# Eight additions of 256 elements in place of three on GpSimd, in the fold of a cross network's second layer

## What is computed

```python
x0 = xk = e                                  # [1024, 39, 16], gathered from 39 tables
for W in (f0, f1, f2):                       # [39*39,128], [128*39,128], [128*39,128]
    z = einsum('bfd,bgd->bfgd', x0, xk)      # every field with every row of the layer before
    cur = einsum('bpd,pm->bmd', z, W)        # 128 new rows
    outs.append(cur); xk = cur
h = concat([sum over d of each cur, dense_ctx])          # [1024, 400]
y = relu(relu(h @ W_top1 + b1) @ W_top2 + b2) @ W_top3   # [1024, 1]
```

## Time and profile before

| | |
|---|---|
| median of three runs | 1338.43 us |
| profiled execution | 1340.8 us |
| its span | 1339.0 us |
| matmul busy | 1281.1 us, 96% of the span |
| VectorE busy | 1149.6 us, 86% |
| ScalarE busy | 915.3 us, 68% |
| GpSimd busy | 1058.3 us, 79% |
| granted TensorE clock, mean | 0.99 of full speed |

### The profile page before, as it was taken

How to read it: one execution, slowest core, us unless ns; L and a number is a source line. 1 busy time by engine, 2 the same in 40 slices (tenths; PEclk the granted TensorE clock), 3 DMA queues, 4 the chain that set the end, 5 groups by cost and what they waited for, 6 DMA issues and landing times. The chain is left out here.

```text
span 1339.0 us, 25654 instructions
## 1 busy us (share of the span) xinstructions
PE 1281.1 (96%) x5983; PEld 1017.3 (76%) x5983; DVE 1149.6 (86%) x3210; ACT 915.3 (68%) x3053; POOL 1058.3 (79%) x743
## 2 busy tenths in 40 slices
PE   4899999999999999999999999999999999999998
PEld 2577777877788777887768877788767887788787
DVE  3499999699888999789986999969998699988983
ACT  2377776677666777577765777757776577766783
POOL 7588888688886888779887788868888688884561
PEclk9699999999999999999999999999999999999999
DMA  7623233322233322223332133330333322333000
GB/s 197 158 54 52 61 64 65 61 41 53 48 61 61 64 54 46 44 56 61 65 65 44 25 63 66 65 63 9 62 64 66 61 40 44 55 61 61 2 3 1
DMA packets 129470, 76.62 MB, mean 57 GB/s; under 512 B 90792, under 2 KB 98201, under 8 KB 129301
## 3 DMA queue, kind: packets, MB, share of 16 engines
q1 hardware_dynamic: 119061, 72.07, 26.5%
q0 software_dynamic: 10240, 2.64, 2.2%
HBM read 68.16 MB, written 3.87 MB: 54 GB/s over the span
## 5 line engine op out<-in xcount | busy, mean ns | idle before, releaser
L394 ACT ACTIVATE parts<-pieces,x_cols 128x128 f32<-128x128 f32 x2560 | 717.9, 377 | 188.3 <-PE pieces L690 159.4
L528 DVE SCALAR_TENSOR_TENSOR parts<-pieces,x_cols,parts 128x128 f32<-128x128 f32 x2432 | 678.7, 339 | 136.8 <-PE pieces L690 99.4
L688 PE MATMUL pieces<-w_hi,cur_hi 128*128 128x512 f32 (+1 forms) x1280 | 549.3, 429 | 29.2 <-DVE parts L528 23.0
L690 PE MATMUL pieces<-w_hi,cur_lo 128*128 128x512 f32 (+1 forms) x1280 | 499.4, 390 | 0.0
L689 PE MATMUL pieces<-w_lo,cur_hi 128*128 128x512 f32 (+1 forms) x1280 | 499.1, 390 | 0.0
L342 POOL TENSOR_TENSOR parts<-parts 128x1024 f32<-128x1024 f32 x127 | 324.2, 2553 | 149.8 <-DVE parts L528 144.4
L333 POOL DMA_INDIRECT emb<-in_table,rows x320 | 345.1, 1079 | 79.7 <-issue 60.9
L688 PEld LDWEIGHTS pieces<-w_hi,cur_hi 128*128 128x128 f32 x1280 | 242.1, 189 | 102.3 <-DVE parts L528 46.4
L690 PEld LDWEIGHTS pieces<-w_hi,cur_lo 128*128 128x128 f32 x1280 | 241.2, 188 | 51.7
L689 PEld LDWEIGHTS pieces<-w_lo,cur_hi 128*128 128x128 f32 x1280 | 242.3, 189 | 47.7
L413 ACT ACTIVATE pairs_hi<-pairs 117x512 fp32r<-117x512 f32 (+1 forms) x224 | 141.9, 634 | 190.9 <-DVE pairs L538 137.3
(11 more groups left out here) (66 smaller groups left out, 597.6 us busy)
## 6 DMA issues: line engine op xcount, KB each, us to landing
partners<-x_wide SPq DMA_DIRECT2D x62, 546.0 KB
partners<-x_wide SPq DMA_DIRECT2D x31, 468.0 KB
x_rep<-x_wide SPq DMA_DIRECT2D x96, 78.0 KB
emb<-in_table,rows POOLq DMA_INDIRECT x320
x_diag<-x_cols SPq DMA_DIRECT2D x256, 10.0 KB
x_wide<-emb SPq DMA_DIRECT2D x32, 80.0 KB
x_wide<-emb SPq DMA_DIRECT2D x32, 32.0 KB
wt<-in_wt SPq DMA_DIRECT2D x1, 1024.0 KB
```

The lines of the kernel that those rows point to most:

```text
L394: last = nc.scalar.activation(parts[n % 2][:, 4 * i + r, :], src[:, r * H:(r + 1) * H], ACT.Copy, scale=x_cols[n // 4][:, n % 4, f:f + 1])
L528: nc.vector.scalar_tensor_tensor(acc, src[:, r * H:(r + 1) * H], x_cols[n // 4][:, n % 4, f:f + 1], acc, ALU.mult, ALU.add).then_inc(acc_d ...
L688: nc.tensor.matmul(dst[:, 0:width], hi[:, cols], w1_hi[:, ws], start=True, stop=False)
L690: nc.tensor.matmul(dst[:, 0:width], lo[:, cols], w1_hi[:, ws], start=False, stop=True).then_inc(l2d_ready if q in D_PIECES else l2a_ready, 1)
```

## The change

GpSimd's three additions per block become eight of 256 elements per partition: four for the first step, in the order of slots 0, 4, 2, 6; two for the second, two for the third. The first four wait for nothing of each other. Each of the other four waits for the addition two places before it, in place of the one just before it. `tree_done` now rises by 8 per block. VectorE's fold of the last block keeps its three instructions and raises the semaphore by 4, 2 and 2. No number that is computed changes.

```diff
-TREE = 3
+TREE = 8
+FOLD = 2
...
-                pool.tensor_tensor(v[:, 0:8], v[:, 0:8], v[:, 8:16], ALU.add).then_inc(tree_done, 1)
-                pool.wait_ge(tree_done, g * TREE + 1)
-                pool.tensor_tensor(v[:, 0:4], v[:, 0:4], v[:, 4:8], ALU.add).then_inc(tree_done, 1)
+                for a in (0, 4, 2, 6):
+                    pool.tensor_tensor(v[:, a:a + FOLD], v[:, a:a + FOLD], v[:, a + 8:a + 8 + FOLD], ALU.add
+                                       ).then_inc(tree_done, 1)
+                for a in (0, 2):
+                    pool.wait_ge(tree_done, g * TREE + a + 2)
+                    pool.tensor_tensor(v[:, a:a + FOLD], v[:, a:a + FOLD], v[:, a + 4:a + 4 + FOLD], ALU.add
+                                       ).then_inc(tree_done, 1)
                 wait(pool, cur2_ready, g - 1)
-                pool.wait_ge(tree_done, g * TREE + 2)
-                pool.tensor_tensor(out4[:], v[:, 0:4], v[:, 16:20], ALU.add).then_inc(tree_done, 1)
+                for a in (0, 2):
+                    pool.wait_ge(tree_done, g * TREE + 5 + a // 2)
+                    pool.tensor_tensor(out4[:, a:a + FOLD], v[:, a:a + FOLD], v[:, a + 16:a + 16 + FOLD], ALU.add
+                                       ).then_inc(tree_done, 1)
```

More of the change, by code:

```diff
@@ L571, in add_last_parts @@
                 dve.wait_ge(acc_done, (g + 1) * D_OPS)
-                nc.vector.tensor_tensor(v[:, 0:8], v[:, 0:8], v[:, 8:16], ALU.add).then_inc(tree_done, 1)
-                dve.wait_ge(tree_done, g * TREE + 1)
-                nc.vector.tensor_tensor(v[:, 0:4], v[:, 0:4], v[:, 4:8], ALU.add).then_inc(tree_done, 1)
+                nc.vector.tensor_tensor(v[:, 0:8], v[:, 0:8], v[:, 8:16], ALU.add).then_inc(tree_done, 4)
+                dve.wait_ge(tree_done, g * TREE + 4)
+                nc.vector.tensor_tensor(v[:, 0:4], v[:, 0:4], v[:, 4:8], ALU.add).then_inc(tree_done, 2)
                 dve.wait_ge(cur2_ready, g - 1)
-                dve.wait_ge(tree_done, g * TREE + 2)
-                nc.vector.tensor_tensor(out4[:], v[:, 0:4], v[:, 16:20], ALU.add).then_inc(tree_done, 1)
+                dve.wait_ge(tree_done, g * TREE + 6)
+                nc.vector.tensor_tensor(out4[:], v[:, 0:4], v[:, 16:20], ALU.add).then_inc(tree_done, 2)
             def halve_tails(u, n):
```

## The result

The changed kernel takes 1384.2 us (median of 4, 1382.4 to 1388.8), the kernel before 1339.3 beside it (4 runs): ratio 1.034, 95% interval 1.031 to 1.037. The forecast was 1354, 16 us more than before; the time lies inside the range of 1322 to 1405, the sign is right, the size is not. The profiled execution took 1384.4 us, its span 1382.5, 43.5 more than before.

The account below looks back on a forecast made before the run. GpSimd (97% taken up) and VectorE were taken as almost full in plain tiles. Terms +6.2, +14, +3.9, -3.5 and -5 gave +15.6, called +16 us: 1354 us against the median of 1338.4, range 1322 to 1405.

Parts of the forecast that it names:

- the tiles of 38.59 us: Tile after the one with the third layer: GpSimd has 4.10 us and more idle, takes up 2.8, so nothing added.
- the fixed parts: Size-independent cost of five more additions per fold: starts 0.66 us apart, 0.2 us more per fold, 0.8 per tile.
- the loop's turn: Where the loop turns, GpSimd idles or catches up: 1 us taken off for each of five turns, -5.
- first quad, tiles 2 to 4: Three tiles of the first quad: 117.0 us against 110.81, +6.2.
- third and fourth tiles, six quads: Last two tiles of each looped quad: GpSimd needs 78.0 us against 75.2, +14 over five; +3.9 in the sixth.
- GpSimd becomes the bound of the plain tiles: GpSimd's load per plain tile rises from 35.97 to 38.8 us, so a plain tile takes 39.0 us.
- The encounters: GpSimd and VectorE taking turns at SBUF: 10 per tile in place of 6.6, 0.42 us each, 2.0 us more per tile.
- VectorE's waits: Single waits shrink to at most 0.7 us but are more numerous: 3.3 us per tile against 3.6, little relief.
- Rival C: VectorE isn't let in between queued additions and waits a whole fold, up to 5.2 us: over 1440 us; chance 0.07.
- A: GpSimd's additions overlap nearly whole, so the change is faster: 1312 us, with half of it 1326; chance 0.26.
- B: GpSimd's additions don't overlap, 0.815 us from start to start: 87 us more, 1425 us; chance 0.12.
- D: Nothing to be measured over the whole kernel, the terms cancel: 1336 to 1341 us; chance 0.09.

Follow-up runs that it names:

- the halved gathers: Every second gather of rows left out: 1312.7 us in the changed kernel (0.979), 1314.9 us in the kernel before (0.981).
- the two added waits: The changed kernel with its fifth and seventh addition each waiting for the one just ahead: 1421.8 us, 1.061 to the kernel before.
- the chained kernel: The changed kernel with each of its eight additions waiting for the one just ahead: 1502.6 us, 1.120 to the kernel before.
- the seven additions: The changed kernel with one of eight additions left out: 1364.9 us queued; 1336.5 us with the fourth and sixth waiting for the one just ahead.

## Why the prediction was right in kind and wrong in size

The step that failed most is the term for the tiles of 38.59 us, put at nothing; behind it come the price of the fixed parts and the 5 us for the loop's turn. The account of the 43.5 us of span, cut at first folds, beside the forecast's terms:

| stretch | before | changed | difference | forecast |
|---|---|---|---|---|
| up to the second tile's first fold | 101.3 | 105.1 | +3.8 | none |
| first quad, tiles 2 to 4 | 110.8 | 119.1 | +8.3 | +6.2 |
| six tiles with the third layer | 280.0 | 278.0 | -2.1 | -3.0 |
| the six after them | 231.6 | 242.5 | +10.9 | 0 |
| third and fourth tiles, six quads | 451.4 | 474.4 | +23.1 | +14 + 3.9 - 5 = +12.9 |
| the rest | 163.8 | 163.4 | -0.4 | -0.5 |

- **GpSimd becomes the bound of the plain tiles**: right. Tiles of 39.0 us were forecast, 39.6 came; its waits for VectorE there are gone, and ScalarE waits 18.7 us for folds where it waited for none. Its sum comes out: GpSimd taken up for 35.97 + 3.4 us (the two next points) and the 0.24 us that stays make 39.6. That eight additions lose by load is shown by the halved gathers (nothing lost); the two added waits (38 us more lost with nearly nobody passed over) show that passing over is not what loses it.
- **The fixed parts**: under-sized. 0.66 us between starts was forecast, 0.69 measured; 5.61 us per undisturbed fold against 5.36, so 0.46 more than before and not 0.2, 1.9 us per tile and not 0.8. Taking all of a memset's overlap off an addition was the error; the bound of 0.815 for a chained one was met by the chained kernel, whose starts lie 0.81 to 0.82 apart.
- **The encounters**: right in the total by luck. 10 per tile at 0.42 us were forecast; 292 in 127 folds are 9.2 per tile, and the fold's mean above the undisturbed one, 6.55 - 5.61 = 0.94 us, is 0.41 for each. But the forecast counted products and subtractions alone, from 6.6 to 10, and these did not become more: 223 before, 222 after, 7.0 per tile. What rose are the small halvings, from 19 to 70, which the forecast left out. The load rose by (6.55 - 5.71) x 4 = 3.4 us per tile, 1.9 of it fixed parts and 1.5 turns; 0.8 + 2.0 = 2.8 were forecast.
- **The tiles of 38.59 us, "nothing"**: this is the step that failed most, 10.9 us. I gave them the 4.10 us of idle time that stands ahead of their first fold. But that time is over when the tile's folds begin; in the changed trace it is still there, 3.89 us, and within the tile GpSimd is as full as in a plain one (37.63 busy of 40.40 against 36.85 of 39.62, both with the gathers' issuing on top). Idle time ahead of a stretch can't be spent by work behind it. GpSimd's waits for VectorE in this tile, before (580.43 to 619.02) and after (602.44 to 642.84), leave 0.8 us within it before and 0.2 after, beside the one that stands ahead:

```profile
POOL parts L342 <- DVE parts L528: 4.9, 2, 4.1
```

```profile
602.44 3.64 POOL L344 TENSOR_TENSOR parts<-parts 128x256 f32<-128x256 f32 x4 [3.89 <-DVE parts L535]
```

```profile
POOL parts L344 <- DVE parts L535: 4.1, 2, 3.9
```

  The first tile, +3.8 with what stands ahead of it, had no term in the forecast at all.
- **The loop's turn, -5**: over-sized. In the five quads that a turn follows, the third tiles take 39.6 us and the fourth ones 39.3, so 0.3 us comes back at each turn and not 1, 1.6 us in all. (In the sixth, which none follows, the fourth tile takes 40.1.) The 1 us had no row for its size and went in the direction that I hoped for.
- **VectorE's waits**: wrong. "A single wait shrinks to at most one addition, 0.7 us" held for nine in ten; the others run to the fold's end, the longest for 2.3 us (an instruction of 2.96). Rival C had this mechanism, at 0.07, for every wait. It came for 30 of 292. And VectorE's small halvings, which I didn't count among the encounters at all, took 44 us of waits for 3. That being passed over costs time is what the seven additions point to (28 us between queued and with two waits); for the changed kernel itself it is not separated from the load, and a plain tile is accounted for there without it.
- **Rivals**: A (starts 0.62 us or less apart) and B (0.81) are both refuted by 0.69, D by the 45 us.

Open: what decides whether VectorE is let in at a boundary between queued additions. In the changed kernel's trace it most often became ready some 0.33 us before an addition's end both where it got in and where it did not. All 30 that were passed over came during the fifth to seventh addition, while the 134 that came during the first four got in at the next boundary; with seven additions 22 of 23 came during the third, so no place in the fold explains both.

## What to carry to other kernels

When an engine is 97% full in a stretch, cost every added instruction at its full distance from start to start there, and look for its idle time inside the stretch, not ahead of it. Finer pieces on GpSimd don't only offer VectorE more turns: each turn is paid by GpSimd (0.41 us here), so splitting is a loss where GpSimd has no room, and with room it gained next to nothing here either (2 us of 1315 with half of the gathers). Taking load off the full engine (half of the gathers: 26 us) was worth far more than any order of its additions.

## What the runs showed that I had not expected

Between GpSimd additions that are queued without a wait between them, VectorE was let in at most boundaries but passed over to the end of the queue in 30 of 292 cases (seven additions: 23 of 202, an instruction of up to 3.67 us). At a boundary where GpSimd had to wait for the addition just ahead, it was never passed over in any of these kernels. A turn costs GpSimd 0.45 us at a queued boundary (an addition then shows 1.18 for 0.74 us), 0.34 at a chained one. And a wait less can make a kernel slower: with the halvings reading one input the kernel before took 12 us more, although 3.4 us of its waits were gone.
